# Conditioned residual kernel: how the token modulation reaches the repeated rows

## The chip, the cores and the metric

The kernel runs on one core of a Trainium2 chip. The metric is the device time of one execution in microseconds (us). Three executions of the kernel before took 1341.11, 1344.43 and 1346.19 us, so its time is the median, 1344.43 us. The execution that was profiled took 1347.22 us, of which the span from the first to the last instruction is 1345.4 us.

Engines are named as in the profile: PE is TensorE (matmuls; PEld is its weight load), DVE is VectorE, ACT is ScalarE, POOL is GpSimd and SP is SyncE, which issues most of the DMAs. ACTq and SPq are the DMA issues of ACT and SP.

## The reference, cut to what matters

x has 8 batches of 1024 tokens of 512 channels. A first layer (an adapter chosen by the language of the batch, with a layer norm) is added to x. The second layer then works on the sum, here called x:

```python
ctx = causal_ema(x, tau_ctx)
wg = jax.nn.sigmoid(jnp.einsum('btc,ec->bte', concat([x, ctx]), Wg) + bg)
gated = x * wg
h1 = jax.nn.gelu(jnp.einsum('btc,hc->bth', x, Wn1) + bn1, approximate=False)
mod = 0.5 + jax.nn.sigmoid(jnp.einsum('bth,dh->btd', h1, Wn2) + bn2)      # 8 numbers for each token
traces = jax.vmap(lambda tau, m: causal_ema(gated * m[..., None], tau))(tau_raws, jnp.moveaxis(mod, -1, 0))
temporal = jnp.einsum('dbtc,dc->btc', traces, softmax(blend, axis=0))
gate = jax.nn.sigmoid(jnp.einsum('btc,ec->bte', temporal, Wtemp) + btemp)
out = jnp.einsum('btc,ec->bte', gelu(jnp.einsum('btc,ec->bte', x, Wsoma) + bsoma) * gate, Wout)
```

A layer norm of out is added to x. The change concerns only how `mod` is brought into the layout that the traces need.

## The kernel before, in words

The 8192 tokens are cut into 16 tiles of 512 tokens. A tile is four blocks of 128 tokens, a block is four spans of 32 tokens (NB = 4, NI = 4, L = 32). Each engine runs its own program over slots k = -1 to 16. In slot k the engines finish tile k - 1 (the temporal gate and the output), work on the gates, the modulation and the traces of tile k, and begin tile k + 1 (the first layer). Slots are about 81 us apart, and each engine's instructions stand in one order written out by hand; they are tied together by semaphores (`wait_ge`).

The traces are built span by span with matmuls. For a block, `repeat_spans` (L359) has SP read the gated values of the block back from DRAM four times, so that partition 4*s + q holds token s of every span; the gated values were stored there by ACT (`store_spans`, L565). DVE multiplies each repeated block by blend weights in four instructions (`products`, L888, recorded as L902), and PE multiplies the results by the triangular decay factors `Arep` (`within_spans`, L1203, recorded as L1217). `Arep` is the decay table `Dpow` times the modulation of each token, and the modulation therefore has to stand in the same repeated layout, as `m_rep`: 128 partitions by 32 numbers. `products` for block two wait for their rows, and SP issues those rows only when the fourth of the products of block zero is done (L364).

In the kernel before the path to `Arep` is this:

- ACT takes a sigmoid and DVE adds 0.5 (L944), which gives `m_nat` (128 by 32, tokens on partitions).
- PE multiplies a table of zeros and ones, `spread`, by `m_nat` in four fp32 matmuls (`spread_modulation`, L1184, recorded as L1189). It stands between the value gates one and two. SP reloads the table, 256 KB, into `T_sb1` once for each tile (`load_spread`).
- DVE multiplies the result by a mask `own_q` (L955), sums four columns into one (L958) and builds `Arep` (L962).
- DVE then goes on with `products(0, 0, 0)`, the logits of gate two, another product, the gating of block two (`gated(2)`), two more products, the logits of gate three and `gated(3)`.

PE's order in the slot is: the value gates zero to three, half of a soma product, the two halves of `within_spans` for block zero, `span_states` (L1193, recorded as L1199, which needs all four blocks of `g`), and so on to block three. Most of PE's other work is recorded as L1026, the line of a helper.

Of the kernel before, what the change touches and what calls it, by code (L numbers as in the profile page):

```python
# [4 lines left out]
P = 128  # L5
BATCHES, SEQ, C = 8, 1024, 512
A = 128
D = 8
# [5 lines left out]
L = 32  # L14
# [26 lines left out]
def cond_resid_kernel(nc, x, xc, own, spread, ids, w1, w2, b1, b2, g0, be0, wg, wn1, wsoma, wtemp, wout, wn2,  # L41
# [10 lines left out]
    with ctx:  # L52
# [12 lines left out]
        def sem(name):  # L65
            return ctx.enter_context(nc.semaphore(name))
# [56 lines left out]
        m_all = U[:, 3, NI - 1, 96:96 + NI * NB * D].rearrange("p (y q) -> p y q", q=NQ)  # L123
# [6 lines left out]
        columns = sb("columns", [P, 11 + NQ])  # L130
        col, alpha_ctx, b1_col, own_q = columns[:, 0:9], columns[:, 9:10], columns[:, 10:11], columns[:, 11:11 + NQ]
# [8 lines left out]
        g_dram = nc.dram_tensor("g_blocks", [NB, P, C], F, kind="Internal").ap()  # L140
        x1_dram = nc.dram_tensor("x1_tiles", [2, P, NB * C], F, kind="Internal").ap()
# [31 lines left out]
        ld_spread = sem("ld_spread")  # L173
# [7 lines left out]
                 "m": 1, "mrep": 1, "S": 1, "Uused": PIECES // 2, "T": 4, "carry": 1}  # L181
# [22 lines left out]
        m_pre, m_ready, Bm_ready, mrep_ready, A_ready = sem("m_pre"), sem("m_ready"), sem("Bm_ready"), sem("mrep_ready"), sem("A_ready")  # L204
        mall_ready = sem("mall_ready")
# [85 lines left out]
        def _(sp):  # L291
# [26 lines left out]
            def first_loads():  # L318
# [5 lines left out]
                sp.dma_start(own_q, own).then_inc(ld_small, 16)  # L324
# [24 lines left out]
            def slot(k):  # L349
                has_prev, has_cur, has_next = parts_of(k)  # L350

                def load_spread():
                    if has_next:
                        sp.wait_ge(full["y"], upto(4, k + 1, NB - 1))
                    else:
                        sp.wait_ge(full["tt"], upto(4, k - 1, NB - 1))
                    sp.dma_start(T_sb1[:, :], spread).then_inc(ld_spread, 16)
# [16 lines left out]
                if has_prev:  # L374
# [11 lines left out]
                    if has_cur:  # L386
                        load_spread()
# [3 lines left out]
                else:  # L391
                    second_loads()
                    load_spread()
                if has_cur:
                    for b in range(NB):
                        repeat_spans(b)
# [82 lines left out]
        def _(act):  # L479
# [6 lines left out]
            def slot(k):  # L486
# [95 lines left out]
                if has_cur:  # L582
# [10 lines left out]
                    store_spans(0)  # L593
                    for b in range(1, NB):
                        open_gate(b)
                        store_spans(b)
# [30 lines left out]
            act.wait_ge(ld_small, 112)  # L627
# [14 lines left out]
        def _(dve):  # L642
# [16 lines left out]
            def small_tables():  # L659

                dve.wait_ge(ld_small, 112)
# [10 lines left out]
                for hh in range(NH):  # L672
                    for n in range(NC):
                        V_.tensor_copy(blend_x[:, hh, n, :].rearrange("p (s q) -> p q s", q=NQ),
                                       blend_c[:, n, hh * NQ:(hh + 1) * NQ].unsqueeze(2).to_broadcast([P, NQ, L]))
# [49 lines left out]
            def slot(k):  # L725
# [205 lines left out]
                if has_cur:  # L931
# [18 lines left out]
                    if k == 0:  # L950
                        for b in range(NB):
                            layer_input(b)
                    gate_logits(1)
                    dve.wait_ge(full["mrep"], upto(1, k, 0))
                    V_.tensor_tensor(m_all, smp[:, 32:32 + NI * NB * D].rearrange("p (y q) -> p y q", q=NQ),  # L955
                                     own_q.unsqueeze(1).to_broadcast([P, NI * NB * NH, NQ]), ALU.mult).then_inc(mall_ready, 1)
                    dve.wait_ge(mall_ready, upto(1, k, 0))
                    V_.tensor_reduce(m_rep.rearrange("p (b i) h -> p i b h", b=NB),  # L958
                                     m_all.rearrange("p (i b h) q -> p i b h q", i=NI, b=NB), AX.X, ALU.add).then_inc(mrep_ready, 1)
                    gated(1)  # L960
                    dve.wait_ge(mrep_ready, upto(1, k, 0))
# [11 lines left out]
                    dve.wait_ge(A_ready, upto(1, k, 0))  # L973
                    products(0, 0, 0)
                    gate_logits(2)
                    products(0, 0, 1)
                    gated(2)
                    products(0, 1, 0)
                    products(0, 1, 1)
                    gate_logits(3)  # L980
# [34 lines left out]
        def _(pe):  # L1015
# [14 lines left out]
            def slot(k):  # L1030
# [214 lines left out]
                if has_cur:  # L1245
# [8 lines left out]
                    spread_modulation()  # L1254
# [35 lines left out]
            pe.wait_ge(ld_small, 112)  # L1290
# [83 lines left out]
```

## Time and profile before

| what | value |
|---|---|
| median of three executions | 1344.43 us |
| lowest and highest | 1341.11 and 1346.19 us |
| profiled execution | 1347.22 us |
| its span | 1345.4 us |
| PE busy | 1305.6 us, 97% of the span, 7580 matmuls |
| DVE busy | 1044.1 us, 78%, 1542 instructions |
| ACT busy | 555.0 us, 41% |
| POOL busy | 460.9 us, 34% |
| granted TensorE clock, mean | 0.995 of full speed |
| DMA packets | 93933, of which 10258 under 512 bytes |

Busy time of an engine is the time in which it executes instructions. Matmuls are pipelined and their ends are modelled, so a busy PE is not a PE at its peak. In a timeline row the first number is the start in us from the start of the span, the second the duration of the row in us, then come engine, line, operation, what is written and what is read. A bracket at its end says how long the engine stood idle before and for whom.

### The profile page before, as it was taken

The numbers are of one execution on the slowest core, as the hardware profiler recorded it, in microseconds if no ns is written. First come the engines' busy times: TensorE is split into PE (matmuls) and PEld (weight loads), VectorE is DVE, ScalarE is ACT, GpSimd is POOL, SyncE is SP. The second block draws the span as 40 slices with busy tenths as digits, with TensorE's granted clock in tenths as the row PEclk, the third lists the DMA queues.
The fourth block names the chain that finished last, engine by engine and source line by source line (L and its number), as shares of the span: only waits on it lengthen the run. The fifth ranks groups of instructions, "written<-read, shape, count | busy, mean of one in ns | idle before, by whom it ended". The sixth has DMA issues, their size and how long they took to land.

```text
span 1345.4 us, 19282 instructions
## 1 busy us (share of the span) xinstructions
PE 1305.6 (97%) x7580; PEld 1015.1 (75%) x7580; DVE 1044.1 (78%) x1542; ACT 555.0 (41%) x892; POOL 460.9 (34%) x364
## 2 busy tenths in 40 slices
PE   4899999999999999999999999999999999999997
PEld 2668778687787878778687787878868787787766
DVE  7988777797778877787787778778687787778575
ACT  3426253343624525254252634426254262534422
POOL 3407144061521606135061531606125061431102
PEclk9899999999999999999999999999999999999999
DMA  7372442715336171352715425173342714325150
GB/s 269 141 241 81 153 161 71 258 40 183 137 105 218 55 244 62 128 196 80 239 40 179 173 86 204 48 235 118 118 165 78 256 66 164 149 86 181 40 181 32
DMA packets 93933, 190.41 MB, mean 142 GB/s; under 512 B 10258, under 2 KB 14994, under 8 KB 89746
## 3 DMA queue, kind: packets, MB, share of 16 engines
q1 hardware_dynamic: 84626, 172.39, 37.7%
q10 hardware_dynamic: 9216, 16.78, 3.3%
q8 instruction: 60, 0.98, 0.3%
q14 instruction: 31, 0.25, 0.1%
HBM read 138.81 MB, written 50.33 MB: 141 GB/s over the span
## 4 chain that ended last, share of the span: by engine, by line
PE 58%; DVE 16%; issue 9%; DMA 7%; ACT 4%; SPq 2%; POOL 1%; DVEq 0%; POOLq 0%
PE ring L1026 40%; DVE U_f L902 7%; PE Tp L1217 5%; DMA g_blocks<-g_f 4%; PE Tp L1026 3%; PE Tp L1228 3%; DMA grep<-g_blocks 3%; SPq L371 2%; DVE stats L837 2%; PE ring L1242 2%; ACT U_f L561 2%; DVE g_f L911 1%; DMA x<-g_blocks 1%; PE ring L1060 1%; PE ring L1063 1%
## 5 line engine op out<-in xcount | busy, mean ns | idle before, releaser
L425 POOL TENSOR_TENSOR Arep_r<-W,Arep_r 128x512 fp32r<-128x512 f32 x14 | 18.2, 1297 | 541.9 <-ACT Arep_r L524 541.9
L902 DVE TENSOR_TENSOR U_f<-grep,w_qs 128x1024 f32<-128x1024 f32 x128 | 150.8, 1220 | 49.2 <-issue 45.2
L571 ACT ACTIVATE g_f<-g_f 128x512 f32<-128x512 f32 x64 | 40.5, 632 | 260.7 <-DVE g_f L907 260.5
L1217 PE MATMUL Tp<-U_f,Arep_f 128*32 128x256 f32 x2048 | 130.0, 384 | 5.5 <-DVE U_f L902 5.3
L452 POOL TENSOR_TENSOR grep_f<-grep_f,beta_row 128x512 f32<-128x512 f32 x64 | 82.1, 1320 | 68.1 <-DMA grep_f<-x_tiles 68.1
L1217 PEld LDWEIGHTS Tp<-U_f,Arep_f 128*32 128x32 f32 x2048 | 56.1, 109 | 65.2 <-DVE U_f L902 23.0
L1026 PE MATMUL ring<-x1T_hi,Wsoma_hi 128*128 128x512 f32 x256 | 103.4, 404 | 0.0
L1026 PE MATMUL ring<-Wg_hi,x1T_hi 128*128 128x512 f32 x256 | 103.3, 403 | 0.0
L1026 PE MATMUL ring<-seq_hi,Wtemp_hi 128*128 128x512 f32 x256 | 101.0, 394 | 0.1
L1026 PE MATMUL ring<-Wout_hi,g_r 128*128 128x512 f32 x256 | 99.9, 390 | 1.1 <-DVE soma_r L758 1.0
L1026 PE MATMUL ring<-Wg_hi,x1T_lo 128*128 128x512 f32 x256 | 100.2, 392 | 0.0
L1026 PE MATMUL ring<-x1T_hi,Wsoma_r 128*128 128x512 f32 x256 | 100.2, 391 | 0.0
L1026 PE MATMUL ring<-x1T_lo,Wsoma_hi 128*128 128x512 f32 x256 | 100.0, 391 | 0.0
L907 DVE TENSOR_TENSOR g_f<-ring,bg_row 128x512 f32<-128x512 f32 x64 | 44.1, 689 | 71.9 <-PE ring L1026 71.6
L1026 PE MATMUL ring<-seq_hi,Wtemp_r 128*128 128x512 f32 x256 | 99.8, 390 | 0.0
L1026 PE MATMUL ring<-seq_lo,Wtemp_hi 128*128 128x512 f32 x256 | 99.8, 390 | 0.0
L1026 PE MATMUL ring<-Wout_hi,soma_r 128*128 128x512 f32 x256 | 99.7, 390 | 0.0
L1026 PE MATMUL ring<-Wg_r,x1T_hi 128*128 128x512 f32 x256 | 99.7, 390 | 0.0
L1026 PE MATMUL ring<-Wg_hi,seq_hi 128*128 128x512 f32 x256 | 99.7, 389 | 0.0
L1026 PE MATMUL ring<-Wout_r,g_r 128*128 128x512 f32 x256 | 99.7, 389 | 0.0
L1026 PE MATMUL ring<-Wg_hi,seq_lo 128*128 128x512 f32 x256 | 99.7, 389 | 0.0
L1026 PE MATMUL ring<-Wg_r,seq_hi 128*128 128x512 f32 x256 | 99.7, 389 | 0.0
(185 smaller groups left out, 3192.8 us busy)
## 6 DMA issues: line engine op xcount, KB each, us to landing
grep<-g_blocks SPq DMA_DIRECT2D x128, 256.0 KB, 3.7
grep_f<-in_xc SPq DMA_DIRECT2D x16, 1024.0 KB, 7.8
grep<-in_x SPq DMA_DIRECT2D x16, 1024.0 KB, 9.3
x_tiles<-x SPq DMA_DIRECT2D x16, 1024.0 KB, 6.9
g_blocks<-g_f ACTq DMA_DIRECT2D x64, 256.0 KB, 3.5
grep_f<-g_blocks SPq DMA_DIRECT2D x64, 256.0 KB, 3.5
x<-g_blocks SPq DMA_DIRECT2D x64, 256.0 KB, 3.9
grep_f<-x_tiles SPq DMA_DIRECT2D x16, 1024.0 KB, 4.8
```

The lines of the kernel that those rows point to most:

```text
L371: sp.dma_start(spans_of(k, b)[q:P:NQ, :, :], g_dram[b].rearrange("(i s) c -> s i c", i=NI)).then_inc(spans_in(k, b)[0], 16)
L425: nc.gpsimd.tensor_tensor(W1_split[:, 1, :, :], W1[:, :, :], W1_split[:, 0, :, :].bitcast(F), ALU.subtract).then_inc(w1lo_ready, 1)
L452: nc.gpsimd.tensor_tensor(x1_back[:, b, :], x1_back[:, b, :], beta1_row[:, :], ALU.add).then_inc(x1b_ready, 1)
L561: nc.scalar.activation(res[:, b, :], res[:, b, :], ACT.Identity, scale=rstd1[:, b:b + 1]).then_inc(scaled_ready, 1)
L571: nc.scalar.activation(g[:, b, :], g[:, b, :], ACT.Sigmoid).then_inc(sig_ready, 1)
L837: V_.bn_stats(stats0[:, b, :], new[:, b, :]).then_inc(ln0_step, 1)
L902: V_.tensor_tensor(U[:, (n + 2) % 4, :, :], spans_of(k, b)[:, :, at], w_qs[:, hh, at].unsqueeze(1).to_broadcast([P, NI, HC]), ALU.mult).th ...
L907: V_.tensor_tensor(g[:, b, :], bank_of("wg", k, b)[:, :], bg_row[:, :], ALU.add).then_inc(pre_ready, 1)
L1026: last = nc.tensor.matmul(dst, lhsT(a, n), rhs(b, n), start=(first and n == begin and m == 0), stop=(final and n == steps - 1 and m == 2))
L1217: last = nc.tensor.matmul(Tp[b % 2][i * L:(i + 1) * L, at], Arep[:, b * NI + i, hh, :], U[:, (n + 2) % 4, i, :], start=(hh == 0 and c == 0 ...
L1228: last = nc.tensor.matmul(Tp[b % 2][:, :], Epow[a][rows, b, :], V[c][rows, :], start=False, stop=(m == 2))
L1242: last = nc.tensor.transpose(ps[:, n * P:(n + 1) * P], T_sb[b % 2][:, n * P:(n + 1) * P], ident[:, :])
```

## The change

The table `spread`, the mask `own_q`, the four matmuls and the two DVE instructions go. ACT stores `m_nat` to a DRAM tensor `m_dram` (16 spans by 32 tokens by 8 numbers, fp32) behind its store of the first gated block. SP waits for that store and then reads `m_rep` back with one DMA of 2048 pieces of two numbers each (8 bytes), ahead of its reads of the repeated spans. DVE waits for the read instead of the matmuls. The order of the eight modulations within a partition changes from h*4 + q to 2*q + h, with the tables to match, so that the two numbers of a piece are neighbours. In DVE's order `gate_logits(2)` and `gated(2)` move ahead of the first product of block zero, and `gate_logits(3)` stands before the fourth product.

```diff
@@ -138,6 +137,7 @@
         rstd0, rstd1, minus_half, ema_last = (rows4[:, n, :] for n in range(4))
         g_dram = nc.dram_tensor("g_blocks", [NB, P, C], F, kind="Internal").ap()
+        m_dram = nc.dram_tensor("m_blocks", [NB * NI, L, D], F, kind="Internal").ap()
         x1_dram = nc.dram_tensor("x1_tiles", [2, P, NB * C], F, kind="Internal").ap()
 
@@ -349,12 +347,10 @@
                 has_prev, has_cur, has_next = parts_of(k)
 
-                def load_spread():
-                    if has_next:
-                        sp.wait_ge(full["y"], upto(4, k + 1, NB - 1))
-                    else:
-                        sp.wait_ge(full["tt"], upto(4, k - 1, NB - 1))
-                    sp.dma_start(T_sb1[:, :], spread).then_inc(ld_spread, 16)
+                def repeat_modulation():
+
+                    sp.wait_ge(m_stored, 16 * upto(1, k, 0))
+                    sp.dma_start(m_rep, m_dram.rearrange("x s (q h) -> (s q) x h", h=NH)).then_inc(ld_m, 16)
 
                 def repeat_spans(b):
@@ -383,15 +379,13 @@
                         sp.wait_ge(U_ready, upto(PIECES, k - 1, PIECES // 2 - 1))
                     sp.dma_start(x1_back[:, :, :].rearrange("p b c -> p (b c)"), x1_dram[(k - 1) & 1]).then_inc(ld_back, 16)
-                    if has_cur:
-                        load_spread()
                     for b in range(NB):
                         sp.wait_ge(res_ready, upto(4, k - 1, b))
...
                 else:
                     second_loads()
-                    load_spread()
                 if has_cur:
+                    repeat_modulation()
                     for b in range(NB):
                         repeat_spans(b)
@@ -591,6 +585,10 @@
                         nc.scalar.activation(Eend[0][:, :], Eend_raw[:, :], ACT.Identity).then_inc(tablehi_ready, 1)
                     store_spans(0)
+                    act.wait_ge(m_ready, upto(1, k, 0))
+                    if has_prev:
+                        act.wait_ge(ld_m, 16 * upto(1, k - 1, 0))
+                    nc.scalar.dma_start(m_dram.rearrange("(b i) s d -> (i s) b d", b=NB), m_nat).then_inc(m_stored, 16)
                     for b in range(1, NB):
                         open_gate(b)
@@ -672,7 +670,7 @@
                     for n in range(NC):
                         V_.tensor_copy(blend_x[:, hh, n, :].rearrange("p (s q) -> p q s", q=NQ),
-                                       blend_c[:, n, hh * NQ:(hh + 1) * NQ].unsqueeze(2).to_broadcast([P, NQ, L]))
+                                       blend_c[:, n, hh:D:NH].unsqueeze(2).to_broadcast([P, NQ, L]))
                 for n in range(NC):
                     last = V_.tensor_copy(blend_x[:, 2, n, :].rearrange("p (j d) -> p j d", d=D),
@@ -951,14 +949,8 @@
                             layer_input(b)
                     gate_logits(1)
-                    dve.wait_ge(full["mrep"], upto(1, k, 0))
-                    V_.tensor_tensor(m_all, smp[:, 32:32 + NI * NB * D].rearrange("p (y q) -> p y q", q=NQ),
-                                     own_q.unsqueeze(1).to_broadcast([P, NI * NB * NH, NQ]), ALU.mult).then_inc(mall_ready, 1)
-                    dve.wait_ge(mall_ready, upto(1, k, 0))
-                    V_.tensor_reduce(m_rep.rearrange("p (b i) h -> p i b h", b=NB),
-                                     m_all.rearrange("p (i b h) q -> p i b h q", i=NI, b=NB), AX.X, ALU.add).then_inc(mrep_ready, 1)
                     gated(1)
-                    dve.wait_ge(mrep_ready, upto(1, k, 0))
+                    dve.wait_ge(ld_m, 16 * upto(1, k, 0))
                     V_.tensor_tensor(Arep[:, :, :, :],
                                      m_rep.unsqueeze(3).to_broadcast([P, NB * NI, NH, L]),
@@ -971,13 +963,13 @@
                                          ALU.subtract).then_inc(tablelo_ready, 1)
                     dve.wait_ge(A_ready, upto(1, k, 0))
+                    gate_logits(2)
+                    gated(2)
                     products(0, 0, 0)
-                    gate_logits(2)
                     products(0, 0, 1)
-                    gated(2)
                     products(0, 1, 0)
+                    gate_logits(3)
                     products(0, 1, 1)
-                    gate_logits(3)
                     gated(3)
                     products(1, 0, 0)
@@ -1181,19 +1173,9 @@
                     last.then_inc(full["m"], 1)
 
-                def spread_modulation():
-
-                    pe.wait_ge(m_ready, upto(1, k, 0))
-                    pe.wait_ge(ld_spread, 16 * upto(1, k, 0))
-                    for i in range(NI):
-                        last = nc.tensor.matmul(smp[:, 32 + NB * D * i:32 + NB * D * (i + 1)], T_sb1[:, i * P:(i + 1) * P],
-                                                U[:, 3, NI - 1, 0:NB * D], start=True, stop=True)
-                    last.then_inc(full["mrep"], 1)
-
                 def span_states():
 
                     pe.wait_ge(Bm_ready, upto(1, k, 0))
-                    pe.wait_ge(mrep_ready, upto(1, k, 0))
                     pe.wait_ge(g_ready, upto(4, k, NB - 1))
                     for b in range(NB):
@@ -1251,7 +1233,6 @@
                     modulation()
                     value_gate(1)
-                    spread_modulation()
                     value_gate(2)
                     value_gate(3)
@@ -1345,16 +1326,14 @@
     taus = np.asarray(condB_tauraws)
     rows = np.arange(P)
-    tau_table = np.concatenate([taus[rows % D][:, None], taus[rows % NQ][:, None], taus[NQ + rows % NQ][:, None],
+    tau_table = np.concatenate([taus[rows % D][:, None], taus[NH * (rows % NQ)][:, None], taus[NH * (rows % NQ) + 1][:, None],
                                 np.broadcast_to(taus[None, :], (P, D)),
                                 np.broadcast_to(np.asarray(L1_cond_tau_ctx).reshape(1, 1), (P, 1))], axis=1)
...
     each = lambda v: c(np.broadcast_to(np.asarray(v)[..., None, :], np.asarray(v).shape[:-1] + (P, C)))
     arrays = {
-        "x": c(xs), "xc": c(xs.transpose(0, 2, 1)), "own": (rows[:, None] % NQ == np.arange(NQ)[None, :]).astype(np.float32),
-        "spread": (np.arange(NI * P)[None, :] // NQ == rows[:, None]).astype(np.float32),
-        "ids": np.asarray(itok_B_0_8).reshape(1, BATCHES),
+        "x": c(xs), "xc": c(xs.transpose(0, 2, 1)), "ids": np.asarray(itok_B_0_8).reshape(1, BATCHES),
         "w1": c(L0_cond_W1), "w2": c(L0_cond_W2), "b1": c(L0_cond_b1), "b2": each(L0_cond_b2),
         "g0": each(L0_cond_gamma), "be0": each(L0_cond_beta),
```

## Rows read from the trace of the kernel before

**Rows 1.** Page, busy time of the engines: us, share of the span, instructions.
```profile
PE 1305.6 (97%) x7580; PEld 1015.1 (75%) x7580; DVE 1044.1 (78%) x1542; ACT 555.0 (41%) x892; POOL 460.9 (34%) x364
```
**Rows 2.** Waits of PE by releaser: us in total, times, longest us.
```profile
PE Tp L1217 <- DVE U_f L902: 5.3, 13, 1.6
PE smp L1199 <- DVE g_f L911: 2.3, 2, 1.4
```
**Rows 3.** Timeline of PE, 473.4 to 476: the spread and the next matmul.
```profile
474.36 0.97 PE L1189 MATMUL smp<-U_f,T_sb_f 128*128 128x32 f32 x8
475.17 0.48 PE L1026 MATMUL ring<-Wg_hi,x1T_hi 128*128 128x512 f32 x1
```
**Rows 4.** Groups by line, PE: busy us, mean ns, idle before.
```profile
L1189 PE MATMUL smp<-U_f,T_sb_f 128*128 128x32 f32 x128 | 15.7, 266 | 1.5 <-DVE U_f L944 1.5
```
**Rows 5.** Timeline of DVE in one slot, 470 to 512.
```profile
471.85 0.17 DVE L944 TENSOR_SCALAR U_f<-U_f 128x32 f32<-128x32 f32 x1
...
475.37 0.29 DVE L955 TENSOR_TENSOR U_f<-smp,columns 128x128 f32<-128x128 f32 x1
475.70 0.29 DVE L958 TENSOR_REDUCE U_f<-U_f 128x32 f32<-128x128 f32 x1
...
476.56 1.22 DVE L962 TENSOR_TENSOR Arep_f<-U_f,Dpow 128x1024 f32<-128x1024 f32 x1
481.12 1.23 DVE L902 TENSOR_TENSOR U_f<-grep,w_qs 128x1024 f32<-128x1024 f32 x1 [3.34 <-issue]
482.26 0.69 DVE L907 TENSOR_TENSOR g_f<-ring,bg_row 128x512 f32<-128x512 f32 x1
482.86 1.22 DVE L902 TENSOR_TENSOR U_f<-grep,w_qs 128x1024 f32<-128x1024 f32 x1
...
488.25 0.69 DVE L911 TENSOR_TENSOR g_f<-g_f,x 128x512 f32<-128x512 f32 x1 [0.70 <-ACT g_f L571]
488.86 2.35 DVE L902 TENSOR_TENSOR U_f<-grep_f,w_qs 128x1024 f32<-128x1024 f32 x2
...
495.28 4.63 DVE L902 TENSOR_TENSOR U_f<-grep,w_qs 128x1024 f32<-128x1024 f32 x4 [0.61 <-DMA grep<-g_blocks]
...
500.43 4.62 DVE L902 TENSOR_TENSOR U_f<-x,w_qs 128x1024 f32<-128x1024 f32 x4
```
**Rows 6.** Timeline of PE, 502 to 507: the last span products of that slot.
```profile
505.11 0.64 PE L1217 MATMUL Tp<-U_f,Arep_f 128*32 128x256 f32 x8 [0.32 <-DVE U_f L902]
```
**Rows 7.** Timeline of that slot: the DMA issues of ACT and SP.
```profile
471.96 0.33 ACTq L567 DMA_DIRECT2D g_blocks<-g_f  x1
...
474.05 2.54 SPq L371 DMA_DIRECT2D grep<-g_blocks  x4
...
487.70 2.55 SPq L371 DMA_DIRECT2D grep<-g_blocks  x4
```
**Rows 8.** The block stores of ACT by line: durations, and us from issue to landing.
```profile
L567 ACTq DMA_DIRECT2D g_blocks<-g_f x64: 326/326/372, 65.2 to 1294.8; - x64
...
DMA to landing us min/median/max: 2.0/3.5/4.9
```
**Rows 9.** DMA, 474 to 476.6 in 40 slices: busy tenths of the 16 DMA engines.
```profile
DMA  0000000000000000000000399999455999986999
```
**Rows 10.** Timeline of SP at the start: a load of 128 rows of 48 bytes.
```profile
1.16 0.38 SPq L321 DMA_DIRECT2D V_hi_f<-in_taus  x1
```
**Rows 11.** DMA, 2.1 to 2.4 in 40 slices: that load's packets.
```profile
DMA  0000121120245575591022333455433323321310
...
DMA packets 144, 0.01 MB, mean 21 GB/s; under 512 B 144, under 2 KB 144, under 8 KB 144
...
q1 hardware_dynamic: 144, 0.01, 30.9%
```
**Rows 12.** DMA, 258.6 to 258.9 (packets of 512 bytes), then 4.98 to 5.83.
```profile
DMA packets 137, 0.10 MB, mean 341 GB/s; under 512 B 1, under 2 KB 132, under 8 KB 133
...
DMA packets 130, 0.01 MB, mean 14 GB/s; under 512 B 126, under 2 KB 126, under 8 KB 130
```

More of the change, by code:

```diff
@@ L38, with cond_resid_kernel @@
 ALS = 12
-def cond_resid_kernel(nc, x, xc, own, spread, ids, w1, w2, b1, b2, g0, be0, wg, wn1, wsoma, wtemp, wout, wn2,
+def cond_resid_kernel(nc, x, xc, ids, w1, w2, b1, b2, g0, be0, wg, wn1, wsoma, wtemp, wout, wn2,
                       bg, g1, be1, cols, taus, bn2, blend, eye, bits, out):
@@ L122, in cond_resid_kernel @@
         m_rep = U[:, 3, NI - 1, 64:64 + NB * NI * NH].rearrange("p (x h) -> p x h", h=NH)
-        m_all = U[:, 3, NI - 1, 96:96 + NI * NB * D].rearrange("p (y q) -> p y q", q=NQ)
         spare0, V_hi = sb_two_ways("V_hi", [P, C])
@@ L129, in cond_resid_kernel @@
         stats = sb("stats", [P, 16 * NB])
-        columns = sb("columns", [P, 11 + NQ])
-        col, alpha_ctx, b1_col, own_q = columns[:, 0:9], columns[:, 9:10], columns[:, 10:11], columns[:, 11:11 + NQ]
+        columns = sb("columns", [P, 11])
+        col, alpha_ctx, b1_col = columns[:, 0:9], columns[:, 9:10], columns[:, 10:11]
         Wn2 = sb("Wn2", [P, D])
@@ L172, in cond_resid_kernel @@
         ld_back = sem("ld_back")
-        ld_spread = sem("ld_spread")
+        m_stored, ld_m = sem("m_stored"), sem("ld_m")
         ld_w1, ld_w2, ld_b2, ld_norm = sem("ld_w1"), sem("ld_w2"), sem("ld_b2"), sem("ld_norm")
@@ L180, in cond_resid_kernel @@
         names = {"h": 1, "temp": 4, "n1": 1, "soma": 4, "trx": 4, "tt": 4, "out": 4, "y": 4, "wg": 4,
-                 "m": 1, "mrep": 1, "S": 1, "Uused": PIECES // 2, "T": 4, "carry": 1}
+                 "m": 1, "S": 1, "Uused": PIECES // 2, "T": 4, "carry": 1}
         full = {n: sem(f"{n}_full") for n in names}
@@ L203, in cond_resid_kernel @@
         y_ready, ln0_step, x1_ready = sem("y_ready"), sem("ln0_step"), sem("x1_ready")
-        m_pre, m_ready, Bm_ready, mrep_ready, A_ready = sem("m_pre"), sem("m_ready"), sem("Bm_ready"), sem("mrep_ready"), sem("A_ready")
-        mall_ready = sem("mall_ready")
+        m_pre, m_ready, Bm_ready, A_ready = sem("m_pre"), sem("m_ready"), sem("Bm_ready"), sem("A_ready")
         pre_ready, g_ready, U_ready, V_ready = sem("pre_ready"), sem("g_ready"), sem("U_ready"), sem("V_ready")
@@ L323, in first_loads @@
                 sp.dma_start(con, bits).then_inc(ld_small, 16)
-                sp.dma_start(own_q, own).then_inc(ld_small, 16)
                 sp.dma_start(ident[:, :], eye).then_inc(ld_small, 16)
@@ L625, in slot @@
                         x1_high(n)
-            act.wait_ge(ld_small, 112)
+            act.wait_ge(ld_small, 96)
             nc.scalar.activation(alpha[:, 0, :], alpha[:, 0, :], ACT.Exp).then_inc(setup_exp, 1)
@@ L659, in small_tables @@
             def small_tables():
-                dve.wait_ge(ld_small, 112)
+                dve.wait_ge(ld_small, 96)
                 link(V_.tensor_reduce(blend_s, blend_c, AX.X, ALU.max))
@@ L1288, in slot @@
                         x1_by_channels(n)
-            pe.wait_ge(ld_small, 112)
+            pe.wait_ge(ld_small, 96)
             pe.wait_ge(blend_ready, 2)
```

## The prediction

> **What bounds the kernel now.** I read the page first: TensorE (PE) is busy 97% of the span, VectorE (DVE) 78% [rows 1]. So an edit that takes PE time away can pay, and an edit on any other engine pays only where PE waits. The list of waits comes next. PE waits little, and what it waits for from slot to slot is DVE's products for the span matmuls, 5.3 us in 13 waits, and twice the gated blocks [rows 2]. The timeline of one slot tells how close that race is. I count in us from T = 471.85, where DVE makes the modulation [rows 5]. The last four products of the slot end at 500.43 + 4.62 = 505.05, T + 33.20, and PE starts the matmuls on the last of them at 505.11, after 0.32 idle [rows 5, 6]. So PE alone would be there at 504.79. DVE's chain in turn hangs on transfers: it stands 3.34 us before the first product at 481.12, for rows that SP began to issue at 474.05, 7.07 us earlier [rows 5, 7]. The view calls that idle time "issue", but the decay factors had been done since 477.78, and no other wait stands ahead of this product than the one for its rows. The kernel is therefore bound by PE and, only some tenths of a us behind it, by the chain store, read back, sixteen products. That chain is what the change lengthens.
>
> **What it removes.** The four fp32 matmuls run as eight instructions; from their first to the next gate matmul 475.17 - 474.36 = 0.81 us pass [rows 3], 16 times, 13.0 us (the group's busy time is 15.7 us, but neighbours overlap [rows 4]). If DVE kept up, PE would be at the last matmuls of the slot at 504.79 - 0.81 = 503.98, T + 32.1, against 505.11 now: at most 1.13 us a slot, 18 us. The two DVE instructions of 0.29 us go from a place behind which DVE stands idle for 3.34 us [rows 5]: nothing, and 0.6 us a slot if DVE had no such gap. The reload of the table is a DMA in an earlier stretch that nobody but the removed matmuls waits for: nothing. One small load at the start goes, one issue of some 0.4 us as in [rows 10], once: I leave it out.
>
> **What it adds, in order.** (1) The store of the modulation. ACT issues it behind the store of block zero, which is issued at 471.96 and takes 0.33 us: T + 0.45. Stores of a block land after 2.0 us at least, 3.5 in the median [rows 7, 8]. The new one has 512 pieces of 32 bytes behind the block's rows on the same queue. I put its landing at T + 3.0 (bounds T + 2.5 and T + 4.0). Behind ACT's new wait stands the sigmoid of gate one, which is due only after T + 3: free.
>
> (2) SP waits for it, with the reads of block zero queued behind. Before, SP issued these at T + 2.20. The read of the modulation is issued at T + 3.0; its packets begin 0.97 us later, as for the small load (issued at 1.16, first packets in the fifth slice, 2.13) [rows 10, 11]. So they begin at T + 4.0.
>
> (3) The read has 2048 pieces of 8 bytes, 128 for each DMA engine, and no row shows such a transfer. D is the time that its packets take. From below: the 144 packets of the small load took 30.9% of 16 engines over 0.3 us, 10.3 ns each, and 128 of these in a row are 1.3 us. From above: those 144 packets need 0.3 us in all, 2.1 ns each, and 137 packets, mostly of 512 bytes, pass in another 0.3 us: 2048 at 2.1 ns are 4.3 us [rows 11, 12]. Worse still, 130 packets that mostly belong to a load of the same 32 bytes into every partition need 0.85 us, 6.5 ns each, which would be 13.4 us [rows 12]. I take D = 3.0: the 2.1 ns contain the engines' staggered starts, so a long transfer should do somewhat better, but 8-byte reads from DRAM hardly run at their own 10.3 ns without gaps.
>
> (4) The rows of block zero are queued behind it on SP's queue. Their packets began at 475.43 (the twenty-third of 40 slices of 65 ns) and the product started at 481.12, 5.69 us later [rows 5, 9]. If they begin where the small pieces end, the first product starts at S = T + 4.0 + D + 5.7 = T + 9.7 + D. SP's own issue sets a floor, T + 3.0 + 0.6 + 7.07 = T + 10.7. For D = 3.0, S = T + 12.7, against T + 9.27 now. The decay factors (1.22 us) are done before that in any case.
>
> The Trainium skill, "DMA: Bandwidth & Descriptors", section "Queues, rings and completion order", says that an engine takes the descriptors of one ring in order, which is what step (4) assumes. No row here shows small pieces ahead of large ones on one queue.
>
> **The reordered products.** Gate two and its gating now lie before S, where DVE is idle. From starts to starts a product takes 1.14 us (481.12 to 482.26), a gate step 0.60 (482.26 to 482.86), and a gating 0.61 (488.25 to 488.86) [rows 5]. From S on: three products 3.42, gate three 0.60, a product 1.14, gating three 0.61, two products 2.28, the states and their low part at 0.60 each, two products 2.28: 11.5 us to the ninth product. SP may issue the rows for it when the fourth is done, S + 5.2, and from first issue to use these took 495.28 - 487.70 = 7.58 us [rows 5, 7]: S + 12.8. I take S + 12.3, since in this slot DVE waited 0.61 for them and in the list of waits PE seldom stands long. From the ninth product to the end of the sixteenth: 505.05 - 495.28 = 9.77. So the chain ends at S + 22.1 (bounds S + 21.3 and S + 22.6), where before it ended at 9.27 + 23.93. The reordering alone is worth 1.8 us of chain.
>
> **The sum.** S + 22.1 = T + 34.8 against T + 33.2: PE gets on 1.56 us later in each slot, though it has 0.81 less to do. 16 slots: +25 us. The profiled execution took 1347.2 us (span 1345.4): it would take 1372. It stands 2.8 us above the median of 1344.4, so the forecast for the median is 1369 us.
>
> **Rivals.** They differ in D and in the landing of the store.
> - *A wash.* D = 1.3: S = T + 11.0, the chain ends at T + 33.1, 0.1 us a slot gained: 1342 us. The freed PE time is all eaten by the wait for the sixteenth product. For it: the packets' own 10.3 ns. Against it: no load in the trace keeps all engines at that pace.
> - *Faster: the round trip hides.* The store lands at T + 2.5, D is about 1, the ninth product starts at S + 11.5. Then the chain ends at T + 10.2 + 21.3 = T + 31.5, before PE's T + 32.1, and PE keeps its freed time: 13 to 18 us, 1330 us. It decides at S below T + 10.8. For it: DVE's idle 3.34 us and the reordering.
> - *Much slower: the pieces are bound one by one,* as in the 32-byte row. D = 13.4: S = T + 23.1, +12.0 us a slot, 1536 us. Anything between D = 4.3 (+2.9 a slot, 1390 us) and this belongs here too. Against it: that load reads one address for all partitions, this one does not. The Trainium skill, "DMA: Bandwidth & Descriptors", section "Measured (HBM→SBUF, 128 partitions, SWDGE, issued from GpSimd)", puts the floor of a small load at 10.5 ns a packet; by that D would be 21.5 us, and an estimate from the page some 1665 us. The 2.1 ns here speak against it.
>
> **How the numbers follow.** Forecast 0.50, wash 0.20, faster 0.15, much slower 0.15. A difference of 0.5% (6.7 us) is what a measurement of this kernel can tell from none. The forecast's own bounds are D from 2 to 4.3 with the spread of the ninth product, 1350 to 1397 us. The range for 8 in 10 takes in the wash and the lower part of the last rival: 1337 to 1405 us. Faster 0.15, same 0.20, slower 0.65.
>
> **What would show it.** The profile after should have no L1189 group and some 41,000 more DMA packets (16 times 2048 and 512); DVE idle ahead of the decay factors and then ahead of the first product, which starts at T + 12 to 13.5; waits of PE for the products of 1 to 2 us in each slot, where 5.3 us in all stood. The forecast is wrong if the packets of the modulation take under 1.5 us or over 5, if the rows of block zero overtake them, or if PE's waits fall on something other than the products and gating three.

## The result, and the profile after

The changed kernel takes 1338.74 us (median of 13 executions, 1332.36 to 1340.74). The kernel before, beside it on the same chip, takes 1343.91 us (13 executions). The ratio is 0.9958, with a 95% interval of 0.9946 to 0.9969: 5 us faster, where 25 us slower was forecast. The profiled execution took 1339.79 us, its span 1338.0 us.

The page after (busy us, share of the span, instructions; then DMA packets) answers to [rows 1]. The L1189 group of [rows 4] is gone, and PE is 8.8 us less busy. 39023 more packets were moved.

```profile
PE 1296.8 (97%) x7452; PEld 1002.8 (75%) x7452; DVE 1037.9 (78%) x1510; ACT 555.0 (41%) x892; POOL 461.3 (34%) x364
...
DMA packets 132956, 186.72 MB, mean 140 GB/s; under 512 B 51330, under 2 KB 56066, under 8 KB 128770
```

PE's waits after (us in total, times, longest), against [rows 2]. The first line is one wait at the start of the span (10.0 us in the kernel before). The second is the products: 3.8 us more than in the kernel before. The waits for the gated blocks (2.3 us) and for the modulation (1.5 us, [rows 4]) are gone.

```profile
PE Tp L1277 <- DVE U_f L675: 10.7, 1, 10.7
PE Tp L1199 <- DVE U_f L900: 9.1, 20, 1.3
```

The instruction that makes the modulation marks the slots. These are its first, second and last start (us), in DVE's timeline of the kernel before and then of the changed one.

```profile
65.06 0.17 DVE L944 TENSOR_SCALAR U_f<-U_f 128x32 f32<-128x32 f32 x1
...
146.74 0.17 DVE L944 TENSOR_SCALAR U_f<-U_f 128x32 f32<-128x32 f32 x1
...
1276.51 0.18 DVE L944 TENSOR_SCALAR U_f<-U_f 128x32 f32<-128x32 f32 x1
```

```profile
68.54 0.17 DVE L942 TENSOR_SCALAR U_f<-U_f 128x32 f32<-128x32 f32 x1
...
151.50 0.17 DVE L942 TENSOR_SCALAR U_f<-U_f 128x32 f32<-128x32 f32 x1
...
1270.65 0.17 DVE L942 TENSOR_SCALAR U_f<-U_f 128x32 f32<-128x32 f32 x1
```

The changed kernel loses 3.48 us ahead of its first slot and 1.28 in that slot. Over the next 14 slots it needs 1119.15 us instead of 1129.77, which is 0.76 us less in each. From the last mark to the end it gains 1.5 more (67.35 instead of 68.89). So there are two effects of opposite sign, and they are in different places. These are readings of one execution each. The first mark alone is a loose measure: two kernels whose start is that of the kernel before have it at 62.73 and 63.32, and five whose start is that of the changed kernel at 65.53 to 69.38. The second mark separates them (table below).

One slot of DVE, with T = 473.13, against [rows 5]:

```profile
473.13 0.17 DVE L942 TENSOR_SCALAR U_f<-U_f 128x32 f32<-128x32 f32 x1
...
477.24 0.69 DVE L909 TENSOR_TENSOR g_f<-g_f,x 128x512 f32<-128x512 f32 x1 [0.70 <-ACT g_f L565]
478.77 1.22 DVE L954 TENSOR_TENSOR Arep_f<-U_f,Dpow 128x1024 f32<-128x1024 f32 x1 [0.85 <-DMA U_f<-m_blocks]
481.36 0.69 DVE L905 TENSOR_TENSOR g_f<-ring,bg_row 128x512 f32<-128x512 f32 x1 [1.36 <-PE ring L1018]
482.74 0.69 DVE L909 TENSOR_TENSOR g_f<-g_f,x 128x512 f32<-128x512 f32 x1 [0.70 <-ACT g_f L565]
483.35 1.22 DVE L900 TENSOR_TENSOR U_f<-grep,w_qs 128x1024 f32<-128x1024 f32 x1
...
494.93 4.62 DVE L900 TENSOR_TENSOR U_f<-grep,w_qs 128x1024 f32<-128x1024 f32 x4
...
500.37 4.62 DVE L900 TENSOR_TENSOR U_f<-x,w_qs 128x1024 f32<-128x1024 f32 x4
```

The first product starts at T + 10.22 and carries no wait of its own. It stands directly behind the gating of block two, and that hangs on PE (the gate's matmuls) and on ACT (its sigmoid). The last product ends at 504.99, T + 31.86. The gating of block two ends some 0.5 us later in about every other slot: over the 16 slots the first product starts at T + 10.20 to T + 11.91, 10.7 in the median, and in one of them only does it wait for its rows.

The DMA issues of ACT and SP in that slot, against [rows 7]:

```profile
473.24 0.33 ACTq L561 DMA_DIRECT2D g_blocks<-g_f  x1
473.66 0.41 ACTq L591 DMA_DIRECT2D m_blocks<-U_f  x1
```

```profile
475.97 0.38 SPq L353 DMA_DIRECT2D U_f<-m_blocks  x1
476.45 3.15 SPq L367 DMA_DIRECT2D grep<-g_blocks  x4
```

The read's packets are in the DMA view from 476.9 to 478.4, in 40 slices of 0.0375 us (busy tenths of the 16 engines). Slices 3 to 36 hold them, from 476.98 to 478.25.

```profile
DMA  0014344534657999999999999999999543110009
...
DMA packets 2066, 0.02 MB, mean 14 GB/s; under 512 B 2064, under 2 KB 2064, under 8 KB 2066
...
q1 hardware_dynamic: 2066, 0.02, 79.1%
```

That makes D 1.3 us for 2048 pieces of 8 bytes. One piece takes its engine 0.791 x 16 x 1.5 us / 2066 = 9.2 ns.

The start of the span, DVE and then POOL. First the kernel before:

```profile
6.60 0.18 DVE L662 TENSOR_REDUCE V_lo_f<-V_lo_f 128x4 f32<-128x32 f32 x1 [6.60 <-DMA bn_row<-in_bn]
...
14.64 0.29 DVE L706 SCALAR_TENSOR_TENSOR g_f<-g_f 128x128 f32<-128x128 f32 x1
...
15.11 1.38 DVE L706 SCALAR_TENSOR_TENSOR g_f<-g_f 128x128 f32<-128x128 f32 x1
...
17.74 1.65 DVE L777 TENSOR_TENSOR W_r<-W_f,W_hi 128x512 fp32r<-128x512 f32 x1
...
15.08 5.44 POOL L439 TENSOR_TENSOR x<-grep,b_row 128x512 f32<-128x512 f32 x4 [14.24 <-DMA grep<-in_x]
```

Then the changed kernel:

```profile
7.29 0.18 DVE L660 TENSOR_REDUCE V_lo_f<-V_lo_f 128x4 f32<-128x32 f32 x1 [7.29 <-DMA bn_row<-in_bn]
...
15.32 1.25 DVE L704 SCALAR_TENSOR_TENSOR g_f<-g_f 128x128 f32<-128x128 f32 x1
...
17.82 1.24 DVE L704 SCALAR_TENSOR_TENSOR g_f<-g_f 128x128 f32<-128x128 f32 x1
...
20.31 1.65 DVE L775 TENSOR_TENSOR W_r<-W_f,W_hi 128x512 fp32r<-128x512 f32 x1
...
15.12 5.07 POOL L433 TENSOR_TENSOR x<-grep,b_row 128x512 f32<-128x512 f32 x4 [14.28 <-DMA grep<-in_x]
```

DVE's first instruction waits for the last of the small loads, the row bn2, which goes to all 128 partitions. DVE can begin 0.69 us later than before, although SP issues that load 0.47 us earlier. DVE's table steps then run one round further into POOL's time, where a step takes 1.25 us instead of 0.29, and the step that rounds the first weights (W_r) starts 2.57 us later. The Trainium skill, "SBUF — State Buffer", section "Who interferes with whom", says that a VectorE instruction with two SBUF inputs contends with a GpSimd instruction that reads SBUF, by an exclusive lock. The stretched steps, each about as long as one of POOL's (5.07 / 4 = 1.27 us), agree with it.

### The profile page after: what moved, and what is told of

Read it like the earlier page. It is cut to its first block, busy times and chain, and to the rows that moved or that the text cites. A ratio compares the mean times of both kernels' runs of the same rounds, so it can differ in the third digit from the quotient of the medians.

```text
span 1338.0 us, 19024 instructions
## 1 busy us (share of the span) xinstructions
PE 1296.8 (97%) x7452; PEld 1002.8 (75%) x7452; DVE 1037.9 (78%) x1510; ACT 555.0 (41%) x892; POOL 461.3 (34%) x364
## 4 chain that ended last, share of the span: by engine, by line
PE 74%; DVE 14%; DMA 5%; issue 2%; ACT 1%; SPq 1%; POOL 0%; DVEq 0%; ACTq 0%; POOLq 0%
PE ring L1018 56%; DVE U_f L900 8%; PE Tp L1199 5%; PE Tp L1018 3%; PE Tp L1210 3%; DMA grep<-g_blocks 2%; PE ring L1224 2%; SPq L367 1%; PE ring L1052 1%; PE ring L1058 1%; PE ring L1055 1%; PE ring L1038 1%; PE Tp L1038 1%; DMA x<-g_blocks 1%; DVE g_f L905 1%
```

## The experiments

Each kernel was timed in five rounds beside the kernel before on the same chip (medians of 1342.82, 1344.04, 1345.33 and 1345.12 us in the four sets). The marks are starts of the modulation in the profiled execution, "14 slots" is the time from the second to the last.

| kernel | median us | ratio to before [95%] | first mark | second mark | 14 slots |
|---|---|---|---|---|---|
| before (profiled) | 1343.91 | | 65.06 | 146.74 | 1129.77 |
| after | 1338.74 | 0.9958 [0.9946, 0.9969] | 68.54 | 151.50 | 1119.15 |
| b_spread2 | 1357.29 | 1.0099 [1.0067, 1.0132] | 63.32 | 144.91 | 1142.17 |
| b_order | 1345.01 | 0.9996 [0.9966, 1.0026] | 62.73 | 143.77 | 1129.38 |
| a_oldorder | 1364.00 | 1.0145 [1.0116, 1.0174] | 65.53 | 150.20 | 1140.06 |
| a_swap | 1342.18 | 0.9997 [0.9982, 1.0012] | 68.07 | 150.12 | 1122.49 |
| a_wide | 1337.19 | 0.9957 [0.9945, 0.997] | 67.12 | 149.18 | 1117.08 |
| a_read2 | 1353.51 | 1.0073 [1.0047, 1.0099] | 66.75 | 151.22 | 1131.33 |
| a_read3 | 1376.81 | 1.0229 [1.0172, 1.0286] | 69.38 | 155.19 | 1152.85 |
| a_own | 1332.77 | 0.9918 [0.9887, 0.995] | 65.09 | 146.49 | 1116.77 |
| b_noown | 1351.74 | 1.0048 [1.0029, 1.0067] | 68.87 | 151.68 | 1129.22 |
| a_bn | 1332.65 | 0.9913 [0.9896, 0.9929] | 62.95 | 145.59 | 1120.33 |
| b_bn | 1344.17 | 0.9993 [0.9979, 1.0007] | 62.54 | 145.33 | 1128.25 |
| a_ownbn | 1332.46 | 0.9905 [0.9887, 0.9922] | not read | not read | not read |

The 14 slots take 1116.8 to 1120.3 us in four kernels with the new path and the new order (after, a_own, a_bn, and a_wide with its wide pieces), and 1128.3 to 1129.8 in the four that do not (before, b_order, b_noown, b_bn). The gain there is 8 to 13 us, whichever pair one takes.

### What the removed matmuls were worth: b_spread2

```diff
-                    for i in range(NI):
+                    for i in (*range(NI), *range(NI)):
```

> The kernel before with the four spread matmuls run twice; nothing else. Theory A, TensorE time in this place is paid in full: 16 times 0.8 to 1.0 us, 13 to 16 us slower, 1357 to 1360 us. Rival: part of it falls into time that TensorE would have waited for DVE's products anyway (5.3 us in all), then 8 to 11 us.

Measured: 13 us slower, and 12.4 us of it in the 14 slots, 0.89 a slot. The group has twice its 128 matmuls and the waits for products are as before, 5.5 us in all (columns as in [rows 4]):

```profile
L1189 PE MATMUL smp<-U_f,T_sb_f 128*128 128x32 f32 x256 | 29.9, 271 | 1.4 <-DVE U_f L944 1.4
```

So PE's time added in this place counts in full, and its removal can give 0.8 us a slot as long as DVE keeps up.

### The order of DVE: b_order, a_oldorder, a_swap

b_order is the kernel before with the new order of DVE, a_oldorder the changed kernel with the old one:

```diff
-                    products(0, 0, 0)
                     gate_logits(2)
-                    products(0, 0, 1)
                     gated(2)
+                    products(0, 0, 0)
+                    products(0, 0, 1)
                     products(0, 1, 0)
-                    products(0, 1, 1)
                     gate_logits(3)
+                    products(0, 1, 1)
                     gated(3)
```

> The kernel before with the new order of the products alone (gate two and its gating ahead of the first product, gate three ahead of the fourth); the four spread matmuls stay. Theory A, the gain is the freed TensorE time and the order only lets DVE keep up: TensorE still has its 0.81 us a slot to do, so the time falls by what TensorE waits for products now, at most 5 us (1339 to 1344 us). Theory B, the order alone brings the gain: the whole 5 us or more, and T to T of the slots as short as in the changed kernel (1119 us from the second to the last slot, where before had 1130).

> The changed kernel with the order of the products as before (first product ahead of gate two). The round trip stays, TensorE's time stays freed. Theory A: the rows of block zero land about T + 9.5 behind the small pieces, and from the first product the old order needs 23.9 us to the last, where the new one needs 21.6; the chain ends at T + 33.4 where TensorE would be at T + 32.1 to 32.6, so most of the freed time is waited away again: 12 to 20 us slower than the changed kernel, 1350 to 1358 us. Rival, the order carries nothing here as it did in the kernel before: 1339 us.

Measured: the new order alone is worth nothing that shows (the interval allows some 4 us either way). With the round trip in place the old order costs 25 us (1.0145 / 0.9958 = 1.019), more than the 12 to 20 expected. In a slot of a_oldorder with T = 558.20, the first product stands at T + 10.15 waiting for its rows, gate two comes behind it, and PE waits once in each slot for a gated block:

```profile
561.28 2.92 SPq L367 DMA_DIRECT2D grep<-g_blocks  x4
...
568.35 1.23 DVE L900 TENSOR_TENSOR U_f<-grep,w_qs 128x1024 f32<-128x1024 f32 x1 [3.55 <-DMA grep<-g_blocks]
```

```profile
PE smp L1181 <- DVE g_f L909: 17.0, 16, 1.4
PE Tp L1199 <- DVE U_f L900: 11.9, 30, 1.6
```

The waits for products grew by 2.8 us only. The new wait, 17.0 us, is that of the span states, which need all four gated blocks: the old order makes gating three late, and that is most of what it costs.

a_swap puts one product back between the two steps of gate two:

```diff
                     gate_logits(2)
-                    gated(2)
                     products(0, 0, 0)
+                    gated(2)
```

> The changed kernel with the first product between gate two and its gating, where VectorE stands idle for 0.70 us for the sigmoid. If the rows of block zero have landed by T + 9.4, the chain gets 0.7 us shorter and the waits of TensorE for products (9.1 us in all) shrink: 1332 to 1337 us. If they land later, the gating of block two, its store and the rows for block two come later: 1340 to 1348 us.

Measured: 3 to 5 us slower than the changed kernel (by the medians, by the ratios), and the ratio loses all of the gain. In the slot with T = 470.98 the product waited for its rows until T + 10.42, with the gating behind it:

```profile
481.40 1.23 DVE L900 TENSOR_TENSOR U_f<-grep,w_qs 128x1024 f32<-128x1024 f32 x1 [1.45 <-DMA grep<-g_blocks]
482.55 0.68 DVE L909 TENSOR_TENSOR g_f<-g_f,x 128x512 f32<-128x512 f32 x1
```

These two kernels also show when the rows of block zero are there, since their first product waits for them in nearly every slot: T + 10.2 and T + 10.1 in the median of the slots. That is some 0.5 us before the median start of the first product in the changed kernel.

### How long the round trip is, and its slack: a_wide, a_read2, a_read3

a_wide reads the same 16 KB as 128 pieces of 128 bytes. The numbers then land in other places, so its output is not the reference's:

```diff
-                    sp.dma_start(m_rep, m_dram.rearrange("x s (q h) -> (s q) x h", h=NH)).then_inc(ld_m, 16)
+                    sp.dma_start(m_rep, m_dram.rearrange("x s d -> (x s d)").rearrange("(p x h) -> p x h", p=P, h=NH)).then_inc(ld_m, 16)
```

> The changed kernel, but the modulation is read back in 128 pieces of 128 bytes instead of 2048 of 8; the numbers land in other places than the reference wants, so the output is not the reference's. Theory A, the 2048 pieces take 1.3 us of transfer, and nearly all of it lies in time that VectorE waits for gate two anyway: landing about 1.8 us after the issue instead of 2.8, time 0 to 4 us less than the changed kernel's 1338.7. Rival, the small pieces are what keeps the gain below the 13 us of freed TensorE time: 1328 to 1332 us.

Measured: the same time as the changed kernel. The read lands 1.7 us after its issue in the median instead of 2.8, and the decay factors no longer wait for it. Yet the first product starts at T + 10.22 again (T = 470.78), and at T + 10.7 in the median of the slots, as in the changed kernel:

```profile
475.50 1.22 DVE L954 TENSOR_TENSOR Arep_f<-U_f,Dpow 128x1024 f32<-128x1024 f32 x1
479.01 0.69 DVE L905 TENSOR_TENSOR g_f<-ring,bg_row 128x512 f32<-128x512 f32 x1 [2.29 <-PE ring L1018]
...
481.00 3.49 DVE L900 TENSOR_TENSOR U_f<-grep,w_qs 128x1024 f32<-128x1024 f32 x3
```

a_read2 and a_read3 read the modulation two and three times, and both consumers wait for all of it:

```diff
-                    sp.dma_start(m_rep, m_dram.rearrange("x s (q h) -> (s q) x h", h=NH)).then_inc(ld_m, 16)
+                    for at in (96, 64):
+                        sp.dma_start(U[:, 3, NI - 1, at:at + NB * NI * NH].rearrange("p (x h) -> p x h", h=NH),
+                                     m_dram.rearrange("x s (q h) -> (s q) x h", h=NH)).then_inc(ld_m, 16)
```

> The changed kernel with the read of the modulation issued three times (the first two go into unused columns); DVE waits for all. Theory A, the round trip has some slack and the rows of block zero queue behind the small pieces: each further read puts 1.3 us of small packets ahead of these rows, the first product comes 2 to 2.6 us later, and since the chain of sixteen products is as long as TensorE's work, TensorE waits 1.5 to 2.6 us in each slot: 1363 to 1380 us. Rival, transfers on this queue overlap or the modulation is needed much later than it lands: under 5 us slower, 1339 to 1344 us.

> The changed kernel with the modulation read from DRAM twice, one read behind the other on SP, the first into an unused place; ScalarE and VectorE wait for both. It asks where the slack of the round trip ends: one read cost what none of 8-byte pieces costs (no difference to the changed kernel with wide pieces), three reads cost 38 us. If each further read delays the rows of block zero by about 1.3 us behind it and the slack in front of gate two is under 1 us, a second read costs 0.5 to 1.3 us in each of 16 slots: 1347 to 1360. If the slack is a whole read or more: 1339 to 1342.

Measured: the second read costs 15 us over the changed kernel, the third 23 more. In a slot of a_read2 with T = 476.58 the first product starts at T + 11.61, and now it waits for its rows:

```profile
479.42 1.70 SPq L354 DMA_DIRECT2D U_f<-m_blocks  x2
481.22 3.46 SPq L369 DMA_DIRECT2D grep<-g_blocks  x4
...
488.19 1.23 DVE L902 TENSOR_TENSOR U_f<-grep,w_qs 128x1024 f32<-128x1024 f32 x1 [0.83 <-DMA grep<-g_blocks]
```

```profile
PE Tp L1201 <- DVE U_f L902: 17.9, 39, 3.8
```

In the median of the slots the rows are there at T + 11.6, 1.5 us later than in a_swap and 0.9 later than the changed kernel's first product (T + 10.7). The 14 slots cost 0.87 us each. So the rows have about 0.6 us of slack behind one read.

Where the 1.5 us arise can be read too. SP is held at the issue of the second read (the two take 1.70 us, where one took 0.38) and comes to the rows at T + 4.64, in the changed kernel at T + 3.32. From SP's first issue of the rows to the product 6.97 us pass here, 7.07 in the slot of a_oldorder and 7.07 in the kernel before. The medians over the slots are 6.9 us with no small pieces ahead (before), 7.0 and 6.9 behind one read (a_oldorder, a_swap), 7.2 behind two and 7.1 behind three. What a further read delays is SP's issue, by 1.2 to 1.4 us in the median, about one D; from that issue on the rows take as long as without it.

### The start: a_own, b_noown, a_bn, b_bn, a_ownbn

a_own is the changed kernel with the small load back in its place, its data unused. b_noown is the kernel before with that load moved out of the first group:

```diff
-                sp.dma_start(own_q, own).then_inc(ld_small, 16)
...
                 sp.dma_start(Wn2[:, :], wn2).then_inc(ld_rows, 16)
+                sp.dma_start(own_q, own).then_inc(ld_rows, 16)
```

The counts that the engines wait for go with it.

> The changed kernel with the small load of the mask at the start put back (nobody reads it). Theory C, the 3.5 us by which the first slot of the changed kernel started later come from the earlier issue of the first large load, which delays the small load of the bias row by 0.7 us, and VectorE's table steps then run beside GpSimd: with the load back the first modulation is made at T = 65 to 66 us instead of 68.5, and the time falls by 3 us, 1335 to 1336 us. Rival, the late start is chance of that execution: same time as the changed kernel, 1338.7 us, and T anywhere between 65 and 69.

> The kernel before, with its smallest first load (the 128x16 selection table) moved from the first group of small loads to the later group of rows, which VectorE waits for only ahead of its first modulation; nothing else. It asks whether one load fewer ahead of the first large one is by itself what made the changed kernel start late. If so: first modulation at 66.5 to 69 us instead of 65.1, W_r step at about 20 instead of 17.7, and 1344 to 1349. If the late start comes from something else in the change: first modulation at 64 to 65.5 and no difference, 1341 to 1345.

Measured: the load put back gains 6 us, and the load moved away costs the kernel before 6 (0.48%). The second mark tells it most plainly: 143.77 to 146.74 in the four kernels that issue the load in its place (before, b_order, b_spread2, a_own), 149.18 to 151.68 in six of the seven that do not, and 155.19 in a_read3, whose slots are longer. The start of DVE's first instruction is less clear cut: 6.60 to 6.87 in the four, 6.86 to 7.75 in the seven. b_noown's start has the changed kernel's shape:

```profile
7.63 0.19 DVE L662 TENSOR_REDUCE V_lo_f<-V_lo_f 128x4 f32<-128x32 f32 x1 [7.63 <-DMA bn_row<-in_bn]
...
20.67 1.65 DVE L777 TENSOR_TENSOR W_r<-W_f,W_hi 128x512 fp32r<-128x512 f32 x1
```

Between 20 and 30 us the granted clock was 0.83 in the kernel before and 0.66 in both of the others (us of the stretch, busy time and instructions of PE, PEld, DVE, ACT and POOL, clock, DMA share, GB/s); before, then after:

```profile
20.00:30.00 10.00, 8.04 (x20) 4.82 (x20) 7.36 (x16) 5.26 (x5) 6.93 (x6) 0.83 0.93 355
```

```profile
20.00:30.00 10.00, 7.38 (x16) 5.03 (x17) 6.46 (x11) 3.43 (x2) 5.55 (x5) 0.66 1.02 370
```

In the changed kernel PE stands idle from 17.7 to 22.6 us for these weights. The clock is at its upper level (2.4 GHz) up to about 22 us and at the lower one (0.50, 1.2 GHz) from 22 to 28. Whether that carries the loss is not shown: a_wide and a_oldorder start late too, by the second mark, with 0.83 in this stretch, and a_bn below is 6 us faster with the changed kernel's clock from 60 to 150 us (0.96 in both).

a_bn and b_bn move the load of the row bn2 to the later group, in the changed kernel and in the kernel before; a_ownbn does both repairs:

```diff
-                sp.dma_start(bn2_row[:, :], bn2.to_broadcast([P, D])).then_inc(ld_small, 16)
...
+                sp.dma_start(bn2_row[:, :], bn2.to_broadcast([P, D])).then_inc(ld_rows, 16)
```

> The changed kernel with the load of the bias row of the modulation moved from the small first loads to the later row loads (it is not used before the first modulation), so that VectorE's table steps begin without it. Theory C: VectorE starts at about 5 us instead of 7.3, its table steps are done before GpSimd starts at 15.1, and the first modulation comes at T = 61 to 64 us instead of 68.5: 1331 to 1334 us, the best of all. Rival, the first slot hangs on the large loads: T = 66 to 68 and 1336 to 1339 us.

> The kernel before, with the broadcast load of the row bn2 moved from the first group of small loads to the later group of rows, as in the changed kernel with the same edit (1332.65 there). It gives the change's worth when neither kernel waits for that row at the start. If the startup loss is the missing small load's alone, this kernel starts as early as that one (first modulation at 62 to 64), reads 1339 to 1344, and the pair differs by the freed TensorE time, 8 to 12 us. If moving the row helps the kernel before not at all while it helped the changed one: first modulation at 65, 1342 to 1345.

> The changed kernel with both repairs of its start: the small selection load put back ahead of the large loads (unused), and the broadcast load of row bn2 moved to the later group. Each alone read 1332.7. If both repair the same thing, the late end of the group of small loads, the two together are worth no more than one: 1330 to 1335. If they add, since one takes a load out and the other holds the large loads back: 1325 to 1330, with the first modulation ahead of 62.5 us.

Measured: a_bn gains 6 us as a_own does, and both together no more. DVE starts at 5.48, its table steps are done ahead of POOL's first instruction (16.04), and the weights are rounded at full pace:

```profile
14.45 0.69 DVE L775 TENSOR_TENSOR W_r<-W_f,W_hi 128x512 fp32r<-128x512 f32 x1
```

In the kernel before the same edit hardly moves the time (0.9993, interval across 1). Its marks, 62.54 and 145.33, lie beside those of b_order and b_spread2, which start as the kernel before does, so they show no lead that had to reach the end; the profiled execution of the kernel before was a late one at its first mark (65.06). a_ownbn's profiled execution took 1344.70 us, 12 above its median, so its rows are not read.

The change at an equal start is then worth 0.9913 / 0.9993 = 0.992, or 11 us. a_own against the kernel before says the same (0.9918), and so does the changed kernel against b_noown (0.9958 / 1.0048 = 0.991, 12 us).

## Why the prediction was wrong

**What bounds the kernel: right.** PE's time counts to the full, with the chain of products close behind.

**Steps (1) and (2), the store: a little too late.** It is issued at T + 0.53 and lands 2.1 us later. SP's read is issued at T + 2.84 instead of T + 3.0 (T + 2.6 in most slots), its packets begin at T + 3.85 instead of T + 4.0, and the rows behind it are issued at T + 3.32 instead of T + 3.6.

**Step (3), D: the failed step.** I took 3.0 us and measured 1.3, the lower bound. The rows I relied on for more were short bursts: the 144 packets of [rows 11] give 2.1 ns each because the engines start one after another and few are busy at once. A transfer of 2048 keeps the 16 engines at 9 tenths for half its time, at 9.2 ns for a piece on its engine, so the 10.3 ns of a single packet was the figure to use. The Trainium skill, "DMA: Bandwidth & Descriptors", section "Measured (HBM→SBUF, 128 partitions, SWDGE, issued from GpSimd)", divides the floor of a 4 KB load, about 0.67 us, by its 64 packets. The estimate of D = 21.5 us carried that quotient on to 2048 pieces as if it were a rate. This trace has 0.62 ns a piece over the whole transfer (1.27 us / 2048), so the quotient of a floor is no rate here; that it lies near the 9.2 ns of a piece on its engine says nothing.

**Step (4), the rows behind it: wrong as well, by 0.7 to 0.9 us.** With D = 1.3 my formula gives T + 11.0; a_oldorder and a_swap show T + 10.2 and T + 10.1 in the median. The formula adds D to the way of the rows. The runs show that the pieces ahead add nothing to it once SP has issued the rows: 6.9 to 7.2 us from issue to product with none, one, two or three reads ahead. What holds is the floor that I had set beside the formula, from SP's issue: T + 3.32 + 7.07 = T + 10.4. My 5.69 us from first packets to product were taken from a slot in which SP was still issuing the four reads; that they overlap the pieces here is the likely reason, and no run tests it. Whether the rows would have queued for the D = 3.0 that I forecast stays open, since no transfer took so long.

**The reordered products: right in length.** From the first product to the end of the sixteenth 21.64 us passed, against 22.1. Its parts were off and made up for each other: the ninth product starts at S + 11.6 and not S + 12.3, since its rows are there (6.3 us after SP's issue), and from it to the end 10.1 us pass, not 9.77. That the order was worth 1.8 us a slot is near what a_oldorder lost (25 us / 16 = 1.6), but by luck: I had it as a shorter chain of products, and most of that loss is PE's wait for the fourth gated block. What I did not see is that gate two's gating ends at T + 10.2 to 10.8 in most slots whatever the transfer does: it is the new tie of the first product, as a_wide shows. It hangs on PE's gate matmuls; in b_order, which keeps the spread matmuls ahead of them, the first product starts at T + 11.2 to 11.7.

**The sum.** With D = 1.3 alone the sum gives the wash, 1342 us; the rest is step (4) and half a us of the products. The chain ended at T + 31.86 and not at T + 34.8, ahead of the T + 32.1 at which PE could be there, and PE ran the last span products of that slot without a wait. So PE kept its freed time: 0.76 us a slot of 0.81. That is the mechanism of the rival "faster", which needed S below T + 10.8. Its price was 13 to 18 us and its time 1330; the change at an equal start did bring 11 to 12. It came by other terms than the rival's, though: D was 1.3 and not about 1. That 1338.7 lies within my range of 1337 to 1405 is luck, since the start took back half of the gain; without that loss the kernel takes 1333 and lies outside.

**The small load, left out of the sum: 5 to 6 us.** "One issue of some 0.4 us, once" had the wrong sign and a tenth of the size. b_noown shows it without the rest of the change. What is shown is that the missing load makes the start late. The steps between (DVE begins later on bn2's row, meets POOL, rounds the first weights later) are read from rows and a_bn fits them, but none was tried alone, and why the row is there later stays open.

## What to carry to other kernels

The 2048 small pieces, spread over all 16 DMA engines, cost about the time of one piece on one engine times the 128 pieces of that engine (128 x 9.2 ns = 1.2 us, measured 1.3); a short burst gave three times as much. It is no general rule: the row of 32 bytes that goes to all partitions has 8 pieces for each engine and takes 0.85 us in [rows 12], with the engines 16.7% busy. A round trip through DRAM can replace work of the bounding engine for nothing if the work behind it is reordered so that something useful stands in the wait; with the old order the same change would have lost 20 us. After an edit that drops a load, look at when the first instruction of each engine can now begin: one line at the start took back half of what the change gained.

## What the runs showed of the hardware that was not expected

- 2048 reads of 8 bytes from DRAM pass in 1.3 us on 16 engines, 9.2 ns for each on its engine; a store of 512 pieces of 32 bytes lands 2.1 us after its issue.
- Up to three such reads ahead of four reads of 256 KB on the same queue delay SP's issue of these (T + 3.1 with one, 4.3 with two, 5.7 with three), but not the 6.9 to 7.2 us from that issue to the product.
- With one small load fewer ahead of it the row for all 128 partitions is issued 0.47 us earlier and still is there later: DVE could begin at 6.86 to 7.75 us in seven kernels, at 6.60 to 6.87 in the four with the load in place.
- DVE steps of 0.29 us on 128x128 take 1.25 to 1.38 us beside POOL's instructions.
